# Products of ones in TensorE's order, ahead of and inside the filling steps of the attention stage

## The reference, cut to what matters

```
x = x + 0.5 * ffn_lora(layernorm(x))
x = x + attention(layernorm(x))          # the stage of this change
x = x + 0.5 * ffn_lora(layernorm(x))
x = x + 0.5 * moe(layernorm(x))
x = x + retention(layernorm(x))
x = x + 0.5 * moe(layernorm(x))

def attention(x):                        # 16 sequences, T = 256, 16 heads of 8 columns
    q, k, v = split(x @ W_attn + b_attn)
    att = q @ k.T / sqrt(8) + rel_bias   # by head, lower triangle only
    y = softmax(att) @ v
    return y @ W_proj + b_proj
```

## Time and profile before

| | us |
|---|---|
| median of three runs (lowest, highest) | 1731.96 (1723.12, 1746.84) |
| the profiled execution's own time | 1735.6 |
| its span, first to last instruction | 1733.8 |
| PE busy in the span | 1537.2 (89%) |
| DVE busy | 1167.2 (67%) |
| ACT busy | 815.3 (47%) |
| POOL busy | 796.3 (46%) |
| mean granted TensorE clock | 0.911 |

### The profile page before, as it was taken

The page is one execution under the profiler, slowest core; times in us unless marked ns, Lnnn a source line. Parts: engine busy times, 40 slices in busy tenths (PEclk is TensorE's granted clock), DMA queues, the critical chain, the costliest instruction groups (busy, mean ns, idle before and its releaser), DMA issues. The chain is left out here.

```text
span 1733.8 us, 36975 instructions
## 1 busy us (share of the span) xinstructions
PE 1537.2 (89%) x10054; PEld 1258.9 (73%) x10054; DVE 1167.2 (67%) x4550; ACT 815.3 (47%) x1995; POOL 796.3 (46%) x1129
## 2 busy tenths in 40 slices
PE   6699999999897757999959999999999686699995
PEld 5477777777587546888847888887888574588884
DVE  6448888888575743555548898988898666255554
ACT  2247777777625213444424555555555431244442
POOL 2246666666524240222217786877787504111111
PEclk9759999999956778999979999999999868899998
DMA  4598000000023010001021111111111001000003
GB/s 126 149 300 225 0 0 0 0 0 0 7 80 116 18 37 14 27 26 27 27 72 42 41 38 38 37 37 37 37 37 38 1 2 37 25 26 27 25 27 110
DMA packets 101116, 82.91 MB, mean 48 GB/s; under 512 B 9820, under 2 KB 88351, under 8 KB 100720
## 3 DMA queue, kind: packets, MB, share of 16 engines
q1 hardware_dynamic: 95178, 69.87, 15.1%
q0 software_dynamic: 4416, 9.58, 1.6%
q10 hardware_dynamic: 1382, 1.83, 0.4%
HBM read 23.71 MB, written 40.75 MB: 37 GB/s over the span
## 5 line engine op out<-in xcount | busy, mean ns | idle before, releaser
L892 DVE SCALAR_TENSOR_TENSOR moe_block_act<-banks,moe_taken,moe_block_gated 128x128 f32<-128x128 f32 x592 | 166.8, 344 | 186.4 <-ACT moe_block_gated L936 179.1
L921 POOL DMA_INDIRECT y_rows<-moe_block_y,moe_taken x74 | 71.4, 965 | 383.2 <-ACT moe_block_y L946 383.2
L1181 DVE CUSTOM_DVE_ANT_0 attn_z<-banks,rel_bias 128x128 f32<-128x128 f32 (+1 forms) x512 | 161.9, 353 | 69.9 <-PE banks L1311 63.1
L1229 POOL TENSOR_TENSOR attn_z<-attn_top,attn_z 128x256 f32<-128x256 f32 x256 | 159.3, 630 | 94.2 <-DVE attn_top L1181 93.4
L1706 ACT ACTIVATE ret_normed<-banks,ret_head_shift,ret_head_rstd 128x128 f32<-128x128 f32 x256 | 103.9, 458 | 157.0 <-DVE ret_head_shift L1620 157.0
L936 ACT ACTIVATE moe_block_gated<-banks 128x512 f32<-128x512 f32 x148 | 88.6, 599 | 159.2 <-PE banks L977 159.0
L993 PE MATMUL banks<-moe_down,moe_block_actT 128*128 x1184 | 156.3, 275 | 0.0
L1258 ACT ACTIVATE attn_prob<-banks 128x384 f32<-128x384 f32 x256 | 125.9, 492 | 50.2 <-PE banks L1318 40.2
L1318 PE MATMUL banks<-ident,attn_z 128*128 128x128 f32 x768 | 144.0, 299 | 0.3 <-ACT attn_z L1253 0.3
L993 PEld LDWEIGHTS banks<-moe_down,moe_block_actT 128*128 128x128 f32 x1184 | 143.8, 192 | 0.3
L975 PE MATMUL banks<-moe_hi,moe_block_x_hi 128*128 x296 | 130.8, 442 | 1.6 <-DVE moe_block_x_lo L882 1.5
(11 more groups left out here) (260 smaller groups left out, 4255.4 us busy)
## 6 DMA issues: line engine op xcount, KB each, us to landing
slots<-moe_pad SPq DMA_DIRECT2D x12, 2304.0 KB, 20.0
ret_twins<-ret_twins SPq DMA_DIRECT2D x256, 64.0 KB, 2.0
moe_taken<-slots SPq DMA_DIRECT2D x74, 72.0 KB, 1.8
moe_back<-y_rows SPq DMA_DIRECT2D x16, 256.0 KB, 5.0
moe_stage<-in_moe_w SPq DMA_DIRECT2D x4, 576.0 KB, 7.1
bias_reversed<-scratch SPq DMA_DIRECT2D x1, 2048.0 KB, 9.6
out<-x_res SPq DMA_DIRECT2D x8, 256.0 KB, 4.5
ret_stage<-in_ret_w SPq DMA_DIRECT2D x16, 96.0 KB, 2.2
```

The lines of the kernel that those rows point to most:

```text
L892: last = dve.scalar_tensor_tensor(act_f[:, i, at], ps_u[:, i, at], taken[:, b % RB, column:column + 1], gated[:, i, at], ALU.mult, ALU.mult)
L1181: last = dve.tensor_tensor_reduce(out=z[:, k % Z, cols], in0=ps_s[:, k % 2, cols], in1=bias, scale=1.0, scalar=-3.0e38, op0=ALU.add, op1=A ...
L1229: pool.tensor_tensor(z[:, k % Z, P:WIDTH], top[:, k % Z, 1:2].to_broadcast([P, WIDTH - P]), z[:, k % Z, P:WIDTH], ALU.subtract).then_inc(s ...
```

## The change

A tile `ones` of 128 x 512 bfloat16 is filled by POOL in the first block of the program. `keep_busy` issues products of it with itself, 128 x 128 weights against 512 columns, into the bank of `ps_heads`; nothing reads them and nothing waits for them. Eighteen are issued at the start of TensorE's attention stage, ahead of the pipeline. A new stage `stay_busy` of lead 28 comes first in each step's order: in the filling steps -28 to -13 it issues four products a step, in steps -12 to -5 three. In the loop it issues nothing. TensorE's pipeline now starts at step -28. Nothing is removed.

```
+def keep_busy(pe, bank_out, ones, times):
+
+    for _ in range(times):
+        pe.matmul(bank_out, ones[:, 0:P], ones[:, :], start=True, stop=True)
...
+        ps_spare = ps_heads
         ps_heads = ps_heads[:, 0:T].rearrange("p (j i d) -> p j i d", j=BATCH_TILES, d=32)
...
+            def stay_busy(it, k):
+
+                if isinstance(it, int) and it == 0 and k < 24:
+                    keep_busy(pe, ps_spare, ones, 4 if k < 16 else 3)
+
+            keep_busy(pe, ps_spare, ones, 18)
             software_pipeline(pe, BATCHES // GU, U, [
-                (24, per_seq(0, project_v)), (23, of_group(0, project_qk)), (21, of_group(1, project_qk)),
+                (28, stay_busy), (24, per_seq(0, project_v)), (23, of_group(0, project_qk)), (21, of_group(1, project_qk)),
...
+        ones = sb("ones", [P, 512], BF16)
...
                     pool.memset(neg_half[:, :], -0.5)
+                    pool.memset(ones[:, :], 1.0)
```

More of the change, by code:

```diff
@@ L1019, with attention_phase @@
 MASKED = -1.0e30
-def attention_phase(nc, tag, banks, used, x_res, ident, neg_half, w, background):
+def attention_phase(nc, tag, banks, used, x_res, ident, neg_half, w, background, ones):
     GU = 2
@@ L1965, in build @@
             flip_bias(nc, banks, used, attn, attn_loaded, bias_spread)
-            attention_phase(nc, "attn", banks, used, x_res, ident, neg_half, attn, fill_slots)
+            attention_phase(nc, "attn", banks, used, x_res, ident, neg_half, attn, fill_slots, ones)
         with ExitStack() as stage_ctx:
```

## The result

| | before | after |
|---|---|---|
| median (lowest to highest), 12 runs each | 1733.8 (1715.9 to 1755.2) | 1737.9 (1729.8 to 1750.0) |
| profiled execution, its span | 1735.6, 1733.8 | 1740.1, 1738.3 |
| ratio after / before, 95% interval | | 1.0068 (1.0038 to 1.0098) |

Forecast were 1722 us, 11 us less in the attention stage, and a range that ends at 1738. The kernel became slower by 0.7%: within 2%, but beyond its interval on the wrong side. The measured median is inside the range by a tenth of a microsecond, which is luck and no merit of the reasoning.

The account below looks back on a forecast made before the run. PE was taken to bound attention, at half clock until 131 us. Unit 8 3.9 us late, then full clock: unit 22 10.0 us early (upper sum 12.3), 11 taken; 1735.6 minus 11 is 1724.6, by median 1721; predicted 1722, range 1707 to 1738.

Parts of the forecast that it names:

- The price and order of the products: Attention filling on PE: 106 products at 0.22 us each; unit 0's scores at 87.7 us, unit 8's at 100.8.
- The upper case of that sum: Attention: products at 0.213 us, `project_qk` at 0.8 and the `project_out` taken off give a gain of 12.3 us.
- first rival: Clock falls briefly ahead of attention, costing under 2 us, about 1726; chance 0.70 together with the forecast without it.
- the short fall ahead: Ahead of attention: three to four microseconds of products at half speed after a 1.05 us gap, costing under 2 us.
- 512-wide products bring it back: From the retention stage at 653 to 656 us: three busy microseconds at 0.50 are enough to raise the clock.
- third rival: Attention filling: products of ones do not count or the clock stays low throughout; 36 us slower, 1772; chance 0.05.
- the fall-back behind the products: Attention: clock rises on the products, then falls again; 3.9 us late, 1739, up to 10 worse; chance 0.12.
- The scores of unit 8 ... those of unit 22: Attention: 14 units took 34.2 us at low clock against 20.4 for like work at full clock, 13.8 us.
- fourth rival: Attention: other executions may stay low longer, each further 40 us worth 16 us; about 1712; chance 0.13.
- The stages behind attention move forward unchanged: Behind attention: later stages keep their length, so the attention gain of 11 us passes to the total.
- Later stages give the time back: Sign of being wrong: attention ends earlier while the stages behind it lose the time again; no size given.

Follow-up runs that it names:

- e2: Kernel before plus the tile of ones and 53 small (16-column) products at the start of retention; total 1752.1 us, retention 471.4 us.
- e5: Kernel before plus the tile of ones and 106 small products in a block of their own behind retention; retention 475.1 us.
- u1: The changed kernel itself, timed once more; median 1740.7 us, ratio to before 1.0103.
- v1: Kernel before, unchanged, profiled again on a chip where the whole program took about 40 us less; attention 397.0 us.
- v4: Changed kernel without the 18 products ahead of the stage, 88 products in all; attention 395.2 us, retention 473.8 us.
- t2: Kernel before plus the tile of ones and 106 small products at the start of retention, timed; median 1739.1 us, ratio 1.0047.
- t4: Changed kernel with two products in each of the first 16 filling steps, one in the next 8; median 1725.3 us, ratio 0.9982.
- t1: Changed kernel plus 22 small products (44 instructions) at the start of retention, timed; median 1725.8 us, ratio to before 1.0005.

## Why the prediction was wrong

- **The price and order of the products: right.** 29 records in 6.42 us are 0.22 each, as taken from the earlier trace rows. The start was 0.5 us later than assumed, and every mark of the sum was met within 1.6 us. (The upper case of that sum, by its own terms, comes to some 11.7 us and not to 12.3; nothing hangs on it.)
- **The first rival and the short fall ahead: did not occur.** The clock held over a gap of 1.26 us. (The row taken for "512-wide products bring it back" is weak for that: of its eleven products only three are 512 columns wide.) That wide products of ones count was right (none of the changed kernel's five profiles is low in the stage), and so the third rival, all low, fell; so did the fall-back behind the products.
- **"The scores of unit 8 ... those of unit 22": the term that was mis-sized.** The gain was worked out against one execution of before. Its low stretch of 65 us lasts 24 to 65 us in eight profiles; against their mean the gain is 1.4 us and not 11 (4.1 against the four profiles of the kernel before as it is). The prediction called the time of the rise chance, and yet let this chance count on one side only, as a fourth rival of a larger gain. The spread of 1723 to 1747 in the three runs stood beside it.
- **"The stages behind attention move forward unchanged": the step that failed.** They did up to 888 us. Retention then took 13 us more (484.7 against a mean of 471.9 over the four profiles of before and e2 and e5), because 212 added instructions moved its loop. I had costed the instructions by their time on PE alone. "Later stages give the time back" stood among the prediction's signs of being wrong, and it is what happened, but no term and no rival of the sum had a price for it.
- Together: -1.4 and +13 make +11.6 us; the ratio of 1.0068 is 11.8 us, but with terms this uncertain so close a match is luck. The medians of 12 lie only 4.1 apart, 6.3 beside u1. How much of this is the spread of the other stages is not settled: the last flip product started between 63.0 and 80.0 us, and between attention and retention 421.6 to 431.9 us passed on the chips other than that of v1 to v4.

## What to carry to other kernels

Take the loss from a low clock from several executions, not from the one that was profiled. Work that keeps the clock up makes the stage steady (attention took 397.6 to 398.0 us in five profiles, against 392.1 to 409.3 with the attention code of before) more than fast. Whether it makes the whole program steadier is not shown: twelve runs of the changed kernel lie within 20 us and twelve of before within 39, but twelve of t2, with the attention code of before, within 16. Filling work belongs only where the engine waits: half the products (t4) had unit 0's scores 6.7 us earlier. And after adding instructions ahead of a hardware loop, look at that loop's jumps and at the instruction packets before crediting any gain: the same change with 44 idle instructions more is 15 us faster (medians of 1725.8 for t1 and 1740.7 for u1).

## What the runs showed of the hardware that was not expected

Code has a place, and it can cost 13 us in 470. Shifts of TensorE's code by 0, 36, 106, 116, 132, 176 and 256 instructions left retention at 469 to 475 us with 60 or 61 instruction packets in the whole program; 212 and 468 made it 483 to 488 us with 78 or 79. The two pairs that lie 256 instructions apart agree, one good (0 and 256) and one bad (212 and 468). A packet holds 0.98 MB / 60 = 16 KB. The Trainium skill, "TensorE: Matmul & The Clock Gate", section "Step-by-step: what each phase is for", gives 64 bytes for a matmul instruction; as an estimate from that figure, 256 of them are one packet, which fits. That the loop's code is fetched again is shown by 30 packets against 12 in the stage, and by 16 against none from 1050 to 1290 us. Why some places bring this about and others don't is not shown. One reading would fit, but no run tests it: a turn's code fills about nine packets (30 less 12, over two turns), and by where it begins in a packet it touches one more or one fewer.

The clock can stay at 0.50 through 34 us in which PE is busy all the time, and in another execution of the same attention code come back after 4 to 5 us of it (e5, from 86 to 90 us). What decides it was not found.
